# A graph attention layer on one core: projection ahead of the searches, the first unit's plan and gathers inside stage one

## The reference

```python
h = jnp.maximum(_layernorm(x, axis=-1), 0.0)
h = jnp.einsum('ni,hif->hnf', h, W)              # 8 heads of 64
s1 = jnp.einsum('hnf,hf->hn', h, a1)
s2 = jnp.einsum('hnf,hf->hn', h, a2)
scores = jax.nn.leaky_relu(s1[:, :, None] + s2[:, None, :], negative_slope=0.2)
scores = jnp.where(adj[None] > 0, scores, -9e15)
out = jnp.einsum('hnm,hmf->hnf', jax.nn.softmax(scores, axis=-1), h)
x = x + jax.nn.elu(out)                          # heads side by side
```

## Time and profile before

| | |
|---|---|
| median of 3 runs | 774.72 us (771.73 to 777.65) |
| the profiled execution | 777.28 us |
| its span, first to last instruction | 775.6 us |
| busy shares of the span | PE 74%, DVE 84%, ACT 62%, POOL 54% |
| moved by DMA | 269.5 MB, mean 347 GB/s |
| mean granted TensorE clock | 0.852 |

### The profile page before, as it was taken

The page is one execution under the profiler, slowest core; times in us unless marked ns, Lnnn a source line. Parts: engine busy times, 40 slices in busy tenths (PEclk is TensorE's granted clock), DMA queues, the critical chain, the costliest instruction groups (busy, mean ns, idle before and its releaser), DMA issues.

```text
span 775.6 us, 9118 instructions
## 1 busy us (share of the span) xinstructions
PE 575.2 (74%) x2184; PEld 408.2 (53%) x2184; DVE 651.3 (84%) x1966; ACT 477.7 (62%) x763; POOL 422.4 (54%) x805
## 2 busy tenths in 40 slices
PE   0479798898888788683767868685777659988672
PEld 0245454554444445353556657474656448776561
DVE  4659979899976776775879999999989988999983
ACT  0678977799898989925645666675655223334322
POOL 6634434353333332227766457657756876788850
PEclk9989899999888888875769888877788879999986
DMA  9999999999999999917999999999999887999994
GB/s 287 420 380 388 402 358 382 411 385 419 421 417 391 422 419 419 423 69 229 399 406 417 410 407 398 399 393 407 402 393 354 216 219 176 229 245 281 307 243 157
DMA packets 62395, 269.50 MB, mean 347 GB/s; under 512 B 12050, under 2 KB 12050, under 8 KB 49876
## 3 DMA queue, kind: packets, MB, share of 16 engines
q1 hardware_dynamic: 33520, 185.81, 59.5%
q0 software_dynamic: 25824, 77.31, 32.8%
q10 hardware_dynamic: 2996, 5.77, 2.0%
HBM read 243.49 MB, written 31.13 MB: 354 GB/s over the span
## 4 chain that ended last, share of the span: by engine, by line
DVE 21%; DMA 11%; POOL 10%; issue 8%; ACT 3%; PE 2%; DVEq 0%; ACTq 0%; POOLq 0%
DVE nodes L1156 9%; DMA nodes<-table,list_column 9%; POOL nodes L909 5%; POOL nodes L904 4%; DVE agg L1168 3%; DVE places L274 2%; ACT result L970 2%; DMA nodes<-table,column 2%; ACT result L972 2%; DVE best L263 1%; DVE to_row L1132 1%; DMA out_dram<-result 1%; DVE result L1176 1%; DVE owner L1097 0%; PE psC L1315 0%
## 5 line engine op out<-in xcount | busy, mean ns | idle before, releaser
L698 PE MATMUL psH<-sb_W,normedT 128*128 128x512 f32 x384 | 231.7, 695 | 0.0
L253 ACT ACTIVATE packed<-adj_rows,eight 128x3072 uint8<-128x3072 int32 x66 | 188.7, 2860 | 0.8
L904 POOL DMA_INDIRECT nodes<-table,column x138 | 137.4, 995 | 68.3 <-issue 39.9
L749 POOL TENSOR_TENSOR nodes<-nodes 128x520 f32<-128x520 f32 x47 | 60.9, 1296 | 154.2 <-ACT nodes L663 154.2
L1331 PE MATMUL psP<-nodes,ident 128*128 128x256 f32 x276 | 105.5, 471 | 50.4 <-issue 43.8
L909 POOL DMA_INDIRECT nodes<-table,list_column x109 | 110.1, 1010 | 57.7 <-issue 29.9
L1156 DVE TENSOR_TENSOR nodes<-nodes,psW 128x2048 f32<-128x2048 f32 (+4 forms) x66 | 138.7, 2141 | 0.0
L699 PEld LDWEIGHTS psS<-sb_Wa,normedT 128*128 128x128 f32 x384 | 80.5, 210 | 107.1 <-issue 107.1
L274 DVE FIND_INDEX8 places<-best,packed 128x8 uint32<-128x96 f32 (+6 forms) x240 | 109.9, 466 | 0.0
L263 DVE MAX8 best<-packed 128x8 f32<-128x96 f32 (+6 forms) x240 | 102.7, 459 | 6.4 <-ACT packed L253 6.4
L1332 PE MATMUL psP<-nodes,ident 128*128 128x264 f32 x276 | 102.1, 458 | 0.0
(11 more groups left out here) (182 smaller groups left out, 882.6 us busy)
## 6 DMA issues: line engine op xcount, KB each, us to landing
adj_rows<-in_adj_dram SPq DMA_DIRECT2D x66, 1536.0 KB, 10.2
nodes<-in_adj_dram SPq DMA_DIRECT2D x30, 1536.0 KB, 12.7
table<-nodes SPq DMA_DIRECT2D x48, 260.0 KB, 8.8
sb_x_rows<-in_x_dram SPq DMA_DIRECT2D x48, 256.0 KB, 9.1
out_dram<-in_x_dram SPq DMA_DIRECT2D x11, 512.0 KB, 11.3
result<-in_x_dram POOLq DMA_DIRECT2D x11, 512.0 KB, 7.9
out_dram<-result ACTq DMA_DIRECT2D x11, 512.0 KB, 4.6
out_dram<-result POOLq DMA_DIRECT2D x6, 512.0 KB, 6.5
```

What stands on the lines that cost most here:

```text
L253: nc.scalar.activation(words.bitcast(mybir.dt.uint8), sb["adj_rows"][buffer_of(i)][:], ACT.Square, bias=sb["eight"][:], scale=-17.0, accum ...
L698: nc.tensor.matmul(psH[:, t % 2], normedT[:, t % 2, kc], sb["W"][:, kc], start=(kc == 0), stop=(kc == KC - 1))
L904: nc.gpsimd.indirect_dma_start(out=nodes[:, node_at[u] + i * w.direct + j], out_offset=None, in_=table, in_offset=bass.IndirectOffsetOnAxi ...
```

## The change

Stage one gets 53 rounds (`ROUNDS`, `LAG` 5). Projection still takes the first 48, one tile each; the searches of tiles 0 to 29 are spread over all 53, so that the last five rounds hold searches alone. Into the end of stage one go, from stage two: the count of edges of tiles 0 to 11 (round 44), the range of the scores, now over all 48 tiles at once, centres and extremes (round 49), bounds for all tiles and the owner masks of units 0 and 1 (round 50), `front` of unit 0 (round 51), the mask of unit 2 and `front` of unit 1 (round 52), with their parts on ScalarE and TensorE; on GpSimd the gathers of unit 0 and the direct gathers of unit 1. The 11 copies of nodes leave SyncE's rounds 2 to 22 and stand last in ScalarE's list of stage one. Stage two begins with the count of the edges of tiles 12 to 29 and with what is left of the plan. Several buffers of stage two now lie in the array `keys`, which the search of tile 0 has left by then.

```diff
 
 FLAG_SPREAD = 60.0
-SEEN = 36
+LAG = 5
+AHEAD, TURNS = 3, 4
...
+def range_of_scores(nc, dve, sb):
+
+    scores = S2(sb).rearrange("p t h -> p h t")
+    nc.vector.tensor_reduce(sb["most"][:, 0:H], scores, AX.X, ALU.max).then_inc(sb["most_ready"], 1)
+    nc.vector.tensor_reduce(sb["most"][:, H:2 * H], scores, AX.X, ALU.min).then_inc(sb["most_ready"], 1)
+
+
...
             dve_items.append(("crowd", t // 2, 4.1))
-    dve_round = spread_over([c for _, _, c in dve_items], TILES)
+    ROUNDS = TILES + LAG
+    dve_round = spread_over([c for _, _, c in dve_items], ROUNDS)
     rounds_of = {t: [r for (kind, what, _), r in zip(dve_items, dve_round) if kind == "scan" and what[0] == t] for t in range(1, EARLY)}
...
-            for t in range(TILES):
-                if t >= 1:
+            for t in range(ROUNDS):
+                if 1 <= t <= TILES:
                     sp.wait_ge(h_copied, t)
                     sp.dma_start(table[(t - 1) * P + 1:t * P + 1], h_rows[:, (t - 1) % HB]).then_inc(stored[(t - 1) % HB], 16)
                 if t + XB < TILES:
@@ -549,10 +775,6 @@
                 for i in range(6, 2 * EARLY + 3):
                     if act_round[occupant(i)] == t:
                         load_adj(sp, sb, adj, i)
-                if t % 2 == 0 and 1 <= t // 2 <= len(COPIED):
-                    copy_nodes(sp, sb, x, out, COPIED[t // 2 - 1])
-            sp.wait_ge(h_copied, TILES)
-            sp.dma_start(table[(TILES - 1) * P + 1:N + 1], h_rows[:, (TILES - 1) % HB]).then_inc(stored[(TILES - 1) % HB], 16)
...
+            def plan_part(t, part):
+
+                if (t, part) == (TILES - 4, 0):
+                    dve.wait_ge(crowd_done, len(shares))
+                    dve.wait_ge(filled, 1)
+                    count_edges(nc, dve, sb, EARLY_KINDS[0:2], 1)
+                if (t, part) == (TILES + 1, 0):
+                    dve.wait_ge(h_copied, TILES)
+                    range_of_scores(nc, dve, sb)
+                if (t, part) == (TILES + 1, 1):
+                    dve.wait_ge(sb["most_turned"], 1)
+                    centres(nc, dve, sb, EARLY_KINDS[0:2])
+                    extremes(nc, dve, sb)
+                if (t, part) == (TILES + 2, 0):
+                    raise_bounds(nc, dve, sb)
+                if (t, part) == (TILES + 2, 1):
+                    own(nc, dve, sb, 0)
+                    own(nc, dve, sb, 1)
+                if (t, part) == (TILES + 3, 1):
+                    front(nc, dve, sb, 0)
+                if (t, part) == (TILES + 4, 0):
+                    own(nc, dve, sb, 2)
+                    front(nc, dve, sb, 1)
+            for t in range(ROUNDS):
                 moments(t + 3)
                 scale(t + 2)
-                if t == SEEN + 1:
-                    dve.wait_ge(h_copied, SEEN)
-                    seen = S2(sb)[:, 0:SEEN].rearrange("p t h -> p h t")
-                    nc.vector.tensor_reduce(sb["most"][:, 0:H], seen, AX.X, ALU.max)
-                    nc.vector.tensor_reduce(sb["most"][:, H:2 * H], seen, AX.X, ALU.min)
-                for (kind, what, _), r in zip(dve_items, dve_round):
-                    if r != t:
-                        continue
+                due = [item for item, r in zip(dve_items, dve_round) if r == t]
+                for m, (kind, what, _) in enumerate(due):
...
-            for t in range(TILES):
-                turned(t)
-                norm(t + 1)
+            for t in range(ROUNDS):
+                if t < TILES:
+                    turned(t)
+                    norm(t + 1)
                 due = [item for item, r in zip(act_items, act_round) if r == t]
+                if t == TILES + 2:
+                    square(nc, act, sb, 0)
+                    square(nc, act, sb, 1)
                 for item in due[:1]:
                     pack(nc, act, sb, *item)
-                if t >= 1:
+                if t == TILES + 1:
+                    act.wait_ge(mean_summed, 1)
+                    nc.scalar.activation(mean_row[:, 0:HF], psH[0:1, 0], ACT.Copy, scale=1.0 / N).then_inc(mean_made, 1)
+                    nc.scalar.activation(mean_row[:, HF:TABLE], psS[0:1, 0, 0:H], ACT.Copy, scale=1.0 / N).then_inc(mean_made, 1)
+                    act.wait_ge(mean_made, 2)
+                    act.dma_start(table[N + 1:N + 2], mean_row).then_inc(sb["mean_stored"], 16)
+                if t == TILES + 2:
+                    facts_out(nc, act, sb, 0)
+                    square(nc, act, sb, 2)
+                if 1 <= t <= TILES:
                     h_out(t - 1)
                 deviation(t + 3)
                 for item in due[1:]:
                     pack(nc, act, sb, *item)
-            h_out(TILES - 1)
+            facts_out(nc, act, sb, 1)
+            for start in COPIED:
+                copy_nodes(act, sb, x, out, start)
 
         @block.tensor
         def _(pe):
...
                 project(t)
+            e, psA, (ps_most, ps_bound) = EARLY_KINDS[1][2], early_sums(sb)[0], plan_sums(sb)
+            most = sb["most"]
+            pe.wait_ge(h_copied, TILES)
+            pe.wait_ge(added, TILES)
+            nc.tensor.matmul(psH[:, 0], sb["ones"][:], sb["node_sum"][:, 0:HF], start=True, stop=True)
+            nc.tensor.matmul(psS[:, 0, 0:H], sb["ones"][:], sb["node_sum"][:, HF:TABLE], start=True, stop=True).then_inc(mean_summed, 1)
             pe.wait_ge(sb["early_listed"], 1)
-            psA, psB = early_sums(sb)
-            nc.tensor.matmul(psA, sb["earlier"][:], sb["listed"][:], start=True, stop=True)
-            nc.tensor.matmul(psB, sb["ones"][:], sb["listed"][:], start=True, stop=True)
+            pe.wait_ge(sb["most_ready"], 2)
+            nc.tensor.matmul(psA[:, 0:e], sb["earlier"][:], sb["listed"][:, 0:e], start=True, stop=True)
+            nc.tensor.transpose(ps_most[:, 0:P], most[:, 0:H], sb["ident"][:])
+            nc.tensor.transpose(ps_most[:, P:2 * P], most[:, H:2 * H], sb["ident"][:]).then_inc(sb["most_turned"], 1)
+            pe.wait_ge(sb["extremes_ready"], 2)
+            nc.tensor.matmul(ps_bound, sb["ones"][0:H, :], sb["ext"][:], start=True, stop=True).then_inc(sb["bound_summed"], 1)
+            look_up(nc, pe, sb, 0)
+            look_up(nc, pe, sb, 1)
...
                     add_up(t - 1)
+            add_up(TILES - 1)
+            for u in range(HB):
+                pool.wait_ge(sb["table_stored"][u], 16 * (TILES // HB))
+            pool.wait_ge(sb["mean_stored"], 16)
+            gather_direct(nc, pool, sb, table, 0)
+            gather_listed(nc, pool, sb, table, 0)
+            gather_direct(nc, pool, sb, table, 1)
...
+                if u >= 2:
+                    gather_direct(nc, pool, sb, table, u)
+                if u >= 1:
+                    gather_listed(nc, pool, sb, table, u)
...
-            front(0)
+            count_edges(nc, dve, sb, EARLY_KINDS[2:3], 2)
             turn(0)
-            own(2)
-            check_early()
-            front(1)
             turn(1)
+            dve.wait_ge(counts_summed, 1)
+            centres(nc, dve, sb, EARLY_KINDS[2:3])
```

523 lines of the change are left out of this document (250 added, 273 removed).

## The result

The changed kernel takes 779.33 us (median of 19 runs, 774.3 to 784.75), the kernel before 774.72 in the runs on the same chip (19 runs, 768.66 to 779.32): a ratio of 1.007 [1.005, 1.009], **slower by 0.7%**, clear of the interval but small. I had forecast 767.5 and a gain; the time lies 0.3 us beyond the range, on the other side. The two profiled executions took 777.28 (before) and 779.06, with spans of 775.6 and 777.1.

The account below looks back on a forecast made before the run. ScalarE was taken to pace stage one, VectorE to end it, unit 2's scores to set the end. Round 47 9.9 us earlier, VectorE's stage one ending at 356.6, unit 2 7.3 earlier: 774.72 becomes 767.5; range 759, one lower, to 779.

Parts of the forecast that it names:

- part three: Opening of stage two: barrier 1.8 us, unit 0's score at 365.6, unit 2 and all after it 7.3 us earlier.
- Unit 2 starts 7.3 us earlier, and so does all that follows: Stage two: unit 2's scores move from 397.62 to 390.3, and the end moves with them, to 767.5.
- gain given back to the loads: Stage two rival: earlier units meet loads at the same rate, new gather stalls, end at 775 in the limit; chance 0.05.
- unit 2 starts 7 us earlier and the end does not: Sign in the stage two profile that the gain is given back to the loads.
- Part one: Stage one with 53 rounds in place of 48: round 47 opens at 320.2 instead of 330.15, 9.9 us earlier.
- free no one who waits: SyncE's early rounds: removing the copies gains nothing, since ScalarE runs its packs back to back there.
- the rounds close up: Rival in rounds 4 to 27: less search shortens them to 121 to 123 us, another 8 to 9 gained, 759; chance 0.22.
- Part two: End of stage one: remaining searches and the plan among them end VectorE's stage one at 356.6, 17.3 us later.
- the wait for the projection: After round 47 opens: VectorE's range of scores waits for the last projection copy-out; 3 to 7 us lost, 3.5 taken.
- The barrier costs 1.8 as now: Between stages one and two: the barrier's cost stays at 1.8 us.
- The copies hold up the gathers: Rival around the barrier: gathers land behind copies, unit 0 at 370 to 371, gain 2 or 3 us, 772; chance 0.18.
- The lower clock: Rival in early rounds: TensorE drops its clock, 4.2 us per such round, five make it 788; chance 0.13.

Follow-up runs that it names:

- e12: Changed kernel with one extra unread VectorE instruction ahead of the scores of each of units 4 to 14, no added bytes; 779.88 us, 1.006.
- e11: Changed kernel with no copies of nodes; x is added to every result on its way out instead; 769.93 us, 0.996.
- e1: Changed kernel with the 11 copies issued by SyncE in rounds 2 to 22 again, gathers kept at the end of stage one; 771.59 us, 0.995.
- e10: Changed kernel with the 11 copies on SyncE, one in every fourth round from 4 to 44; 769.06 us, 0.995.
- e3: Changed kernel with copies back in SyncE's rounds 2 to 22 and all gathers behind the barrier; 779.54 us, 1.008.
- e9: Changed kernel with the 11 copies on SyncE, one in each of rounds 1 to 11; 773.30 us, 1.000.
- e5: Kernel before the change with only its 11 copies moved to the end of ScalarE's list, no gathers ahead; 782.91 us, 1.013.
- e2: Changed kernel with all gathers behind the barrier, copies still at the end of ScalarE's list; 774.86 us, 1.000.
- e4: Changed kernel with the 11 copies issued by SyncE at the start of stage two, ahead of its loads; 778.57 us, 1.003.
- e8: Changed kernel with the 11 copies on SyncE in round 48, behind the projection's last store and ahead of three loads; 780.61 us, 1.010.
- e13: Changed kernel with copies for tiles 0 to 11 only, on SyncE in every fourth round 4 to 24, remaining x added later; 767.25 us, 0.991.
- e6: Changed kernel without the 11 copies and the wait for them, so that transfer of x is left out; 765.72 us, 0.990.

## Why the prediction was wrong

**The failed step** is the last of part three: "Unit 2 starts 7.3 us earlier, and so does all that follows." Its first half holds. Unit 0 was forecast at 365.6 and came at 364.8, unit 2 at 390.3 and came at 391.5. The second half does not: I read that VectorE "hardly waits" behind unit 2 and took that for its being the bound. In the changed kernel it is the DMA engines that are the bound up to unit 17 (share 0.98, and 1.01 behind 360; e12 and e11); for the kernel before, where the share is 0.97 and 1.02, that is argued from share and bytes, since the added work was not tried there. The earlier trace rows already showed 0.99, 0.99 and 1.01 for stage one, a column I used for sizes only. An earlier unit 2 asks for the same bytes sooner from engines that are full, and the lead is taken back at gathers: 4.00, 1.58 and 4.70 us before units 3, 7 and 15 (2.03 before unit 15 in the kernel before, and 0.6 before unit 7).

The first of these waits, the largest part of the lost lead, comes from the barrier as well. I followed the gathers as far as unit 2 (its wait was 0.81). Unit 3's last gather took 20.4 us, and that is not new: before, it had up to 21.0 (388.56 to 409.53). But GpSimd issued it at 387.1, only 1.5 us earlier than before. Ten gathers done ahead save it 12.5 us at one per 1.25, and the late barrier took 11 of them: it issues almost without a pause from 359.1 on, as it had from 351.5 before. In e11, where the barrier opens at 344.6, the same gather goes out at 372.1 and unit 3 waits for nothing. The rival *gain given back to the loads* is what happened, at 0.05 the one with the least chance, and its limit of 775 was still too good. Of the signs I named, "unit 2 starts 7 us earlier and the end does not" is the one that came (6.1 earlier, the span 1.5 longer).

**The sum came near up to unit 2 by two errors that cancel, which is luck.** Part one: round 47 at 305.1, not 320.2. e1 splits these 15 us, since it has the 53 rounds with the copies where they were: round 47 opens there at 315.6. So 10.5 are the copies taken off SyncE's early rounds (5 to 14 by e10, e3 and e9, at 310.2, 314.3 and 318.6, and 9.2 by themselves in e5), which I had said "free no one who waits", and 4.6 are left of my sum. ScalarE's timeline in e1, with the openings of rounds 4, 17, 18 and 28:

```profile
56.42 0.61 ACT L898 ACTIVATE normedT<-psT 128x512 f32<-128x512 f32 x1
...
124.51 0.60 ACT L898 ACTIVATE normedT<-psT 128x512 f32<-128x512 f32 x1
...
131.11 0.61 ACT L898 ACTIVATE normedT<-psT 128x512 f32<-128x512 f32 x1
...
187.53 0.62 ACT L898 ACTIVATE normedT<-psT 128x512 f32<-128x512 f32 x1
```

Rounds 4 to 27 take 131.1 in it, as forecast (130.8), and round 17, the second of two empty ones, 6.60 (6.7). In the changed kernel they take 125.6, and that round 5.03 (119.49 to 124.52), because the copies are gone. The rival *the rounds close up* gave round 47 at 312 or less as its sign. The sign came, but not for its reason, less search in a round: with the copies in place rounds 4 to 27 did not close up, and the 4.6 lie before round 4 (1.5) and in rounds 28 to 46 (128.0 against 131.5).

Part two: from round 47 to the last rank VectorE took 35.5 us against 36.4 forecast, with 4.22 for the wait for the projection against 3.5, so the last rank came at 340.6 and not at 353 to 360. Part three: "The barrier costs 1.8 as now" failed by 16 us (17.95). The cause is the gathers at the end of GpSimd's list with the copies in flight, shown by e1, e2 and e4.

A reading on which the change rests was off too: between 339.3 and 365.72 VectorE does not mostly wait for the plan's chain. It is busy for 13.5 of these 26.4 us, and its waits are 7.55 for gathers, 1.79 at the barrier and only 2.9 for TensorE and ScalarE.

**The other rivals.** *The copies hold up the gathers* was right in its mechanism (17.6 to 19.2 us from issue to landing beside them, 3.7 in e1) and wrong in its place: the wait is at the barrier, where all engines stand, and unit 0 itself waited for no gather. The Trainium skill (DMA: Bandwidth & Descriptors, Queues, rings and completion order) says that an engine takes turns between queue rows packet by packet. I had worked out from it that these gathers land near 3.7; the measurement decides against that conclusion, and whether the engines take turns so, no run here shows. *The lower clock* did not come: 0.99 in rounds 4 to 27 (0.94 before) and 0.92 in rounds 28 to 46 (0.84 before), while TensorE was busy for 95% and 82% of these stretches (89% and 81% before). The rule of the Trainium skill (TensorE: Matmul & The Clock Gate, What's actually happening), that activity releases the throttle, agrees with that.

**What stays open.** The bytes left at 360 us, at one rate of 395 GB/s for all, give unit 17 within 1.4 us in nine of the fourteen traces. In e3, e5, e8, e12 and e13 it comes 2.4 to 4.9 us later, since they move 388 to 391, and why is not known; bytes alone do not rank the versions to a few us. Part of the 4.6 us between the medians, against 1.5 between the spans and 1.8 between the profiled executions, is only this: single executions scatter by about 1%. And e3, the plan ahead with neither gathers nor copies moved, is slower than before (1.008) with a unit 2 that is 4.4 us earlier; its waits of 2.25, 1.49 and 3.39 us before units 4, 6 and 14 fit the account, but I did not test them apart. By the ratios the gathers ahead gain 1.2% with the copies early (e1 against e3) and lose 0.7% with the copies late (after against e2).

## What to carry to other kernels

Before costing an earlier start, ask of each stage which resource is full, and count DMA among the engines: where its share is 0.98 over hundreds of us, a gain is bytes moved in the idle stretch or bytes not moved at all, and VectorE at 92% with hardly a wait may still be following. Two signs tell the cases apart: add harmless work to the busy engine (here 8.9 us did not move the ratio), and compare MB moved up to a fixed unit. And put no gathers at the end of GpSimd's list before a barrier while bulk transfers are in flight.

## What the runs showed of the hardware

- GpSimd's end of list waits until its gathers have landed: the barrier opened 4.3, 4.5, 6.0, 6.6, 18.7, 18.9 and 22.3 us after the issue of the last gather (e1, e4, e13, e10, after, e12, e8) as the last two gathers took 3.7, 3.8, 4.8, 5.1, 17.6, 18.0 and 20.6 to land. Copies of ScalarE in flight did not hold it (e2, 342.8).
- A gather of 128 rows lands 3.7 us after issue with no bulk transfer beside it (e1), and 17.6 to 19.2 beside copies of 512 KB (after). In stage two, beside loads of 1536 KB, the medians from 360 to 590 us are 14.0 to 14.5 (before) and 15.3 to 16.1 (after), and those that VectorE waited for took 20.4 (after, unit 3) and 23.6 (e6, unit 2).
- A small store behind copies on the same queue came when they had landed: the mean row's, issued at 341.9, released its gather at 350.9, and the last copy, issued at about 336, took 14.4 us to land (e5). Loads behind copies took 30 to 39 us (e8). No run had such a store on another queue beside the copies, so the order of the queue and the load of the engines are not told apart.
- Copies of 5.77 MB from DRAM to DRAM cost 14.4 us of span at the end of stage one (after against e6), 16.4 at the start of stage two (e4 against e6), and 7.3 to 9.4 in the rounds of stage one (e1, e9 and e10 against e6). By the ratios of many runs it is 1.7%, 1.3% and 0.5 to 1.1%, so 13, 10 and 4 to 8 us.
